# Row transfers sent without pauses, a shared chunk split around the first expert transposes, diagonal tiles made earlier

## The reference

```python
x = _layernorm(x + attention(x, Wq, bq, Wk, bk, Wv, bv, Wo, bo))     # x: (4, 512, 256)
router_logits = x @ w_gate                                          # 8 experts
probs = softmax(router_logits)
topk_w, topk_ids = top_k(probs, 2)
topk_w = topk_w / sum(topk_w)
gu = einsum('th,ehf->etf', x, w_gate_up)                            # w_gate_up: (8, 256, 256)
eo = einsum('eti,eih->eth', silu(g) * u, w_down)                    # g, u: the halves of gu
routed = einsum('te,eth->th', combine, eo)                          # two experts for each token
shared = (silu(x @ w_sh_g) * (x @ w_sh_u)) @ w_sh_down              # 512 inner columns
x = _layernorm(x + routed + shared)
```

## Time and profile before

| | before |
|---|---|
| median of 3 runs | 249.2 us (248.55 to 251.33) |
| the profiled execution: its time, its span | 249.33 us, 247.5 us |
| PE busy | 226.2 us (91%) |
| DVE busy | 148.7 us (60%) |
| POOL busy | 137.0 us (55%) |
| ACT busy | 116.2 us (47%) |
| PE's part of the chain that ended last | 81% |
| mean granted TensorE clock | 0.979 of 2.4 GHz |

### The profile page before, as it was taken

One profiled execution on the slowest core, in us unless ns is written; L12 is line 12 of the kernel. 1 busy time (PEld: TensorE's weight loads), 2 busy tenths in 40 slices (PEclk: granted clock), 3 DMA queues, 4 the chain that ended last, 5 costly groups with the idle time before them and its releaser, 6 DMA issues.

```text
span 247.5 us, 5128 instructions
## 1 busy us (share of the span) xinstructions
PE 226.2 (91%) x1440; PEld 195.1 (79%) x1440; DVE 148.7 (60%) x526; ACT 116.2 (47%) x298; POOL 137.0 (55%) x163
## 2 busy tenths in 40 slices
PE   7999999999899999999996699999999979999950
PEld 2578898798789889788994688888888867899950
DVE  2853462376555948659844666665666631699960
ACT  2272603932380731572342266776777752422460
POOL 0067688899788675566672045666656563003260
PEclk9999999999999999999999799999999999999995
DMA  5954763321411220221543235555555411982242
GB/s 169 371 180 109 229 196 83 97 82 39 127 47 43 88 87 0 88 84 65 205 162 82 69 113 166 148 160 153 166 162 150 131 51 11 381 214 79 86 162 93
DMA packets 21580, 31.72 MB, mean 128 GB/s; under 512 B 3248, under 2 KB 14257, under 8 KB 21556
## 3 DMA queue, kind: packets, MB, share of 16 engines
q1 hardware_dynamic: 17552, 22.46, 30.7%
q0 software_dynamic: 3456, 8.43, 9.9%
q10 hardware_dynamic: 548, 0.53, 0.6%
HBM read 19.70 MB, written 12.76 MB: 131 GB/s over the span
## 4 chain that ended last, share of the span: by engine, by line
PE 81%; DVE 8%; ACT 3%; issue 2%; DMA 2%; POOL 0%; POOLq 0%; DVEq 0%
PE bank L335 21%; PE bank L337 19%; PE bank L336 19%; PE bank L622 4%; PE bank L377 3%; PE bank L526 3%; DMA xt_raw<-in_xT 2%; PE bank L455 2%; PE bank L391 2%; PE bank L645 2%; PE bank L444 2%; PE bank L500 1%; PE bank L414 1%; PE bank L405 1%; PE bank L352 1%
## 5 line engine op out<-in xcount | busy, mean ns | idle before, releaser
L1404 POOL DMA_INDIRECT y_pairs<-x_t,dst x40 | 38.9, 973 | 36.9 <-DVE dst L1198 14.1
L1359 POOL DMA_INDIRECT x_slots<-x,slot x32 | 31.5, 984 | 15.9 <-DMA x_slots<-x,slot 7.7
L335 PE MATMUL bank<-wf_hi,ot_hi 128*128 x80 | 26.6, 333 | 2.4 <-DVE ot_lo L1200 1.9
L335 PE MATMUL bank<-x1t_hi,wf_hi 128*128 128x512 f32 x64 | 26.0, 407 | 0.7 <-DVE xt_raw L1052 0.5
L337 PE MATMUL bank<-x1t_hi,wf_lo 128*128 128x512 f32 x64 | 25.2, 395 | 0.0
L336 PE MATMUL bank<-x1t_lo,wf_hi 128*128 128x512 f32 x64 | 25.2, 393 | 0.0
L1340 POOL TENSOR_TENSOR wf_lo<-stage,wf_hi 128x512 fp32r<-128x512 f32 x18 | 23.1, 1284 | 1.4
L337 PE MATMUL bank<-wf_hi,ot_lo 128*128 x80 | 23.1, 289 | 0.0
L336 PE MATMUL bank<-wf_lo,ot_hi 128*128 x80 | 23.0, 287 | 0.0
L738 ACT ACTIVATE k_sb<-bank,cst 128x256 f32<-128x256 f32 x16 | 7.7, 480 | 30.6 <-PE bank L352 28.6
L1198 DVE SCALAR_TENSOR_TENSOR dst<-o_sb,te_f 128x1 f32 (+1 forms) x40 | 9.1, 226 | 21.0 <-ACT ot_hi L853 21.0
(11 more groups left out here) (181 smaller groups left out, 681.8 us busy)
## 6 DMA issues: line engine op xcount, KB each, us to landing
o_sb<-x_slots SPq DMA_DIRECT2D x40, 129.0 KB, 2.1
stage<-in_wffn SPq DMA_DIRECT2D x18, 256.0 KB, 2.7
x<-in_x SPq DMA_DIRECT2D x4, 512.0 KB, 6.7
out<-x SPq DMA_DIRECT2D x8, 256.0 KB, 2.1
xt_raw<-in_xT SPq DMA_DIRECT2D x3, 512.0 KB, 6.4
x_slots<-fill SPq DMA_DIRECT2D x9, 129.0 KB, 2.9
x<-in_watt SPq DMA_DIRECT2D x4, 256.0 KB, 6.2
k_sb<-y_pairs SPq DMA_DIRECT2D x2, 512.0 KB, 3.8
```

Source lines behind the costliest of these rows:

```text
L335: mm(o, w_hi, m_hi, start=start, stop=False, **more)
L1359: pool.indirect_dma_start(out=x_scat, out_offset=bass.IndirectOffsetOnAxis(ap=slot[:, j, t:t + 1], axis=0), in_=x1[:, t, :], in_offset=Non ...
L1404: pool.indirect_dma_start(out=y_scat, out_offset=bass.IndirectOffsetOnAxis(ap=dst[:, j:j + 1], axis=0), in_=ey[:, u, :], in_offset=None, b ...
```

## The change

Four things change.

- **POOL.** The function `landed` and its five calls are gone; all row transfers are issued one behind the other. `x1_norm(3)` and `x1_lo(2)` change places, and both second-half transfers of batch 1 now stand ahead of them.
- **PE.** The last shared chunk ahead of the experts, `shared_gu(2, 1)`, is split: part 0, then the transposes of tiles 0 and 1, then part 1, then tile 2's transpose. `e_gate_up(1)` and the wait for `sh_out` move ahead of tile 3's transpose. The ring's third and fourth tiles change PSUM banks, so that tile 2's transpose no longer writes a bank of that shared chunk.
- **ACT.** The silu and the rounding of that chunk stand between the roundings of tiles 1, 2 and the first silu; `e_silu(1)` moves ahead of the rounding of tile 3.
- **DVE.** The eight diagonal tiles are made between `shared_out(1, 0)` and `shared_out(1, 1)`; the chunk's multiplication and subtraction stand behind the remainders of tiles 1 and 2.

```diff
-            return bank[(4, 7, 3, 6)[u]][:, 0:KD * P]
+            return bank[(4, 7, 6, 3)[u]][:, 0:KD * P]
...
             shared_dn(1, 1)
-            shared_gu(2, 1)
...
             expert0, expert1, expert2 = experts_of(0)[RING - 1:]
+            shared_gu(2, 1, part=0)
             e_transposed(0, 0, 1)
             e_transposed(1, 1, 1)
-            pe.wait_ge(S["sh_out"], EARLY_B * CS + AHEAD)
+            shared_gu(2, 1, part=1)
+            pe.wait_ge(S["sres_out"], EARLY_B * 2)
             e_transposed(2, 2, 1)
             e_gate_up(0, 0, expert0)
-            pe.wait_ge(S["sres_out"], EARLY_B * 2)
+            e_gate_up(1, 1, expert1)
+            pe.wait_ge(S["sh_out"], EARLY_B * CS + AHEAD)
             e_transposed(3, 3, 1)
-            e_gate_up(1, 1, expert1)
             e_h_transposed(0, 0)
...
-            for c in range(AHEAD):
-                shared_sg(2, c)
-                shared_hh(2, c)
+            shared_sg(2, 0)
+            shared_hh(2, 0)
...
             e_x_hi(1, 1)
+            shared_sg(2, 1)
             e_x_hi(2, 2)
+            shared_hh(2, 1)
             e_silu(0, 0)
+            e_silu(1, 1)
             e_x_hi(3, 3)
-            e_silu(1, 1)
...
             shared_out(1, 0)
-            shared_out(1, 1)
-            shared_h(2, 1)
-            shared_lo(2, 1)
...
+            shared_out(1, 1)
             e_x_lo(0, 0)
             e_x_lo(1, 1)
+            shared_h(2, 1)
             e_x_lo(2, 2)
+            shared_lo(2, 1)
             e_h(0, 0)
+            e_h(1, 1)
             e_x_lo(3, 3)
-            e_h(1, 1)
...
             scatter(0, 1)
-            landed(0, 1)
             scatter(1, 0)
+            scatter(1, 1)
+            x1_norm(3)
             x1_lo(NB - 2)
-            x1_norm(3)
-            landed(1, 0)
-            scatter(1, 1)
-            landed(1, 1)
             scatter(2, 0)
-            landed(2, 0)
             scatter(2, 1)
-            landed(2, 1)
             scatter(3, 0)
             scatter(3, 1)
```

More of the change, by code:

```diff
@@ L1131, in weights, with e_x_lo, e_h, e_h_lo @@
                 dve.wait_ge(S["wtop_out"], 1)
+            def e_x_lo(j, u):
+                dve.wait_ge(S["xe_hi_out"], j + 1)
+                v.scalar_tensor_tensor(dst[:, bass.ds(j, 1)], xg[:, u, D + 1:DT], te_f[:, bass.ds(j + (RING - 1), 1)],
+                                       xg[:, u, D:D + 1], ALU.not_equal, ALU.add).then_inc(S["dst_out"], 1)
+                v.tensor_tensor(xe_lo[:, u, :, :], xe_bank(u).rearrange("p (k n) -> p k n", k=KD),
+                                xe_hi[:, u, :, :].bitcast(F32), ALU.subtract).then_inc(S["xe_lo_out"], 1)
+            def e_h(j, u):
+                dve.wait_ge(S["eg_out"], j + 1)
+                v.tensor_tensor(eh[:, u % 2, :], bank[u % 2][:, IM:2 * IM], eg[:, u % 2, :], ALU.mult
+                                ).then_inc(S["eh_out"], 1)
+            def e_h_lo(j, u):
+                dve.wait_ge(S["he_hi_out"], j + 1)
+                v.tensor_tensor(he_lo[:, u % 2, :], h_bank[:, 0:P], he_hi[:, u % 2, :].bitcast(F32),
+                                ALU.subtract).then_inc(S["he_lo_out"], 1)
             for b in range(NB - 1):
@@ L1361, in scatter @@
                                                 in_=x1[:, t, :], in_offset=None).then_inc(S[f"scattered{b}"], 16)
-            def landed(b, part):
-                pool.wait_ge(S[f"scattered{b}"], 16 * TOPK * (TB // 2) * (part + 1))
             split_x_lo(1)
```

## The result

| | before | after |
|---|---|---|
| median of 20 runs each | 249.34 us (248.5 to 251.74) | 248.55 us (246.85 to 249.92) |
| ratio of the two, 95% interval | | 0.9946 (0.992 to 0.9973) |
| the profiled execution: its time, its span | 249.33 us, 247.5 us | 248.62 us, 246.8 us |
| DVE busy | 148.7 us | 155.4 us |

VectorE was busy for 6.7 us more with the same 526 instructions, a first hint. The kernel became faster by 0.5%, some 1.3 us by the ratio (0.8 us between the medians, 0.7 between the two profiled executions), where 3.8 us were forecast; 248.55 lies above the range of 244.2 to 247.7. The lines of the changed kernel are shifted by about two: `ix_f` in `top_two` is line 1036 (before 1034), `hot` 1040 (1038), `slots` 1092 (1090), `x1_lo` 1348 (1346), the row transfers 1361 (1359), the tiles' transposes 621 (622), the mark 644 (645).

The account below looks back on a forecast made before the run. PE bounds nearly everywhere, but idles at the hand-over to the experts, on late tile loads and VectorE's chain. Moving the experts' first inner-product transpose from 141.19 to 137.36 gains 3.8 us: median 245.4 us, range 244.2 to 247.7.

Parts of the forecast that it names:

- the mark: PE's first transpose of an expert's inner product, at the experts' start: forecast to move from 141.19 to 137.36, 3.8 us.
- The step that failed: POOL, `x1_lo(2)` moved behind `x1_norm(3)`: 2.52 us long, ends at 100.9, wanted by nobody before ACT's copy; no cost.
- POOL's transfers: POOL without pauses: row transfers every 1.27 us; batch 3's first at 115.2 instead of 119.00, last starting at 124.1.
- the rival of stretched transfers: POOL: unpaused row transfers, stretched to 2.0 us each, hold up the last norm; 257 us; 4 in 100.
- The gate: SP's wait for pad and row transfers before the first tile loads: ends at 128.3 instead of 130.43, by the pads.
- The statement of the Trainium skill on HBM's load: SP's last pad, with less company, lands in about the shortest time, 2.0 us; sum some 0.9 us lower.
- The gate that doesn't move: SP's wait before the tile loads still ends at 130.4; reordering alone gives 1.7 us, 247.5 us; 12 in 100.
- PE and ACT at the hand-over: From the shared chunk to the experts: part 1 starts at 132.75, VectorE free 4.29 later, first expert inner-product transpose at 137.36.
- the clock rival: PE's clock stays low at the hand-over to the experts: about 0.9 us back, 246.3 us; 8 in 100.
- DVE's diagonal tiles: DVE between the two `shared_out(1)`: 1.57 us, from 128.55 to 130.1, free while DVE waits for PE until 130.14.
- that case: DVE without its wait before the second `shared_out(1)`: diagonal tiles cost their 1.57 us in front of the first remainder.
- The sum: Whole kernel: first transpose of an expert's inner product 3.8 us earlier, 249.33 to 245.5 us, expected median 245.4.

Follow-up runs that it names:

- the pads on two queues: Changed kernel with `x1_lo(2)` back ahead of `x1_norm(3)` and pad transfers of experts 4 to 7 issued by ACT: 247.07 us against 249.08 (0.9896); chip 3 ratio 1.03.

## Why the prediction was wrong, by its own steps

**The step that failed** is the sentence on POOL that `x1_lo(2)` "ends at 100.9 and is wanted by nobody" before ACT's copy. It ended at 98.26 + 2.55 = 100.81, as forecast, and nobody waited for its result. So its new place was priced at nothing, and no term of the sum stands for what it does to the instructions beside it. It held up `ix_f` and `hot` for 1.95 us; PE, which had 0.50 us of idle time there, got 1.78 more and ran at 1.2 GHz behind it. The trace divides the 3.26 us between `nw` and `slots(3)` in two: up to `slots(2)` (103.85 - 96.36 = 7.49 against 101.98 - 96.45 = 5.53) 1.96 us, and from there to `slots(3)` (14.17 against 12.87) 1.30, close to the 1.4 us that the low clock was seen to cost there. Everything behind is the forecast plus that, to within 0.2 us at the mark (140.80 - 137.36 = 3.44).

**The trace of before had shown it.** I had looked at `x1_lo(2)` in its old place only, where it runs beside an operation of VectorE with a PSUM input (L1016) and holds up nothing. Line 1034 for all four batches reads:

```profile
L1034 DVE CAST ix_f<-top_i x4: 172/184/1237, 59.7 to 111.9; 128x8 f32<-128x8 uint32 x4
```

A median of 184 ns and a longest of 1237. The longest is batch 0's. DVE there:

```profile
59.69 1.24 DVE L1034 CAST ix_f<-top_i 128x8 f32<-128x8 uint32 x1
60.97 0.64 DVE L1038 TENSOR_TENSOR hot<-cst,ix_f 128x32 f32<-128x32 f32 x2
61.64 1.21 DVE L1041 TENSOR_TENSOR hot_m<-hot 128x32 bf16<-128x32 f32 x1
```

and POOL:

```profile
59.62 1.28 POOL L1340 TENSOR_TENSOR wf_lo<-stage,wf_hi 128x512 fp32r<-128x512 f32 x1
60.85 0.61 POOL L1338 CAST wf_hi<-stage 128x512 fp32r<-128x512 f32 x1
61.54 1.26 POOL L1340 TENSOR_TENSOR wf_lo<-stage,wf_hi 128x512 fp32r<-128x512 f32 x1
```

Each group of VectorE's operations ends just behind the one of POOL beside it, and PE waited 1.21 us for `hot_m` there. In the Trainium skill, SBUF — State Buffer, section "Who interferes with whom", says that GpSimd shares a pair of SBUF ports with VectorE under an exclusive lock, and that a VectorE instruction with two SBUF inputs contends with a GpSimd instruction that reads SBUF; the later one waits for the whole of the earlier. The trace agrees for `hot` and `hot_m`, which read two operands in SBUF (1.33 us instead of 0.29, 1.21 instead of 0.19). `ix_f` reads only one, so that sentence doesn't cover it; it was held all the same, 1.11 us instead of 0.20. The prediction had weighed this page only in the other direction, VectorE against GpSimd's descriptors.

**POOL's transfers: right.** Batch 1's eight ran back to back from 85.65 to 95.46 (forecast 85.6 to 95.8). All 32 took 956 to 1262 ns, median 961, as before, so the rival of stretched transfers is refuted on this chip. Batch 3's first started 0.45 behind the start of its `slots` cast and the last 9.16 behind the first (forecast 0.35 and 8.9). In place of the pauses of the earlier trace rows POOL waits three times for `slots`, 8.1 us in all.

**The gate: right in kind, and its size held.** SP's line 294 took 28 ns instead of 1732: the wait ended at 131.6, by the last pad. The pads after:

```profile
L291 SPq DMA_DIRECT2D x_slots<-fill x8: 332/338/947, 119.9 to 129.0; - x8
...
DMA to landing us min/median/max: 2.6/3.1/3.4
```

The last pad landed 2.61 us behind its issue; I had taken 2.9. The statement of the Trainium skill on HBM's load (DMA: Bandwidth & Descriptors, "Latency and other measured facts") would have had it at the shortest time of before, 2.0; the trace doesn't agree. In the kernel with `x1_lo(2)` put back, it was 2.96. The gate that doesn't move is refuted: counted from `slots(3)`, the first load goes out 14.52 us behind it, before 16.48; forecast 14.35.

**PE and ACT at the hand-over: right**, to 0.02 us between part 1 and the mark. That closeness is part luck: VectorE was done with the chunk 4.38 us behind part 1's start (4.29 forecast), and the mark followed 0.25 behind that instead of 0.32. The granted clock was 1.00, so the clock rival is refuted there; a low clock came in another place.

**DVE's diagonal tiles: free, but not for the reason given.** The forecast put them into VectorE's wait ahead of the second `shared_out(1)`, 13.7 us behind the start of the cast of `slots(3)` (128.55 - 114.85). They ran 15.8 us behind it, at 133.83, for 1.65 us, and that wait was gone: VectorE had come late, held for 3.05 us in `w_top` (last section). As the forecast says for that case, they stood in front of the first remainder, which started at 136.12, though its rounding was ready at 135.54. It cost nothing because PE took up the first expert's gate and up only at 137.79.

**The sum.** Gain in the hand-over 26.34 - 22.78 = 3.56 us (forecast 3.8), lost ahead of it 3.26: 0.3 to 0.4 at the mark, 0.7 at the span's end. The two profiled executions differ by as much (249.33 - 248.62 = 0.71); the ratio of all the runs gives 1.3 us with an interval from 0.7 to 2.0, so the traces account for the lower end of it, and one trace of each can't say whether there is more. With the failed step taken out on the chip, the time is 246.37: inside the range, 1.0 us above the forecast. There the gain at the mark is (18.42 + 22.96) against (18.40 + 26.34) = 3.36, and 1.7 us of it are lost again behind the mark (108.0 against 106.3). The granted clock was 0.66 from 200 to 205 us there, where the kernel before and the one with the pads on two queues show 1.00. An estimate from that row: 5 x (1 - 0.66) = 1.7 us of full speed are missing. The low clock of the last stretch (225 to 244 us) is not the cause: it is 0.85 there and 0.82 with the pads on two queues, which loses nothing between the mark and the end. Why the clock fell at 200 us in the one kernel and not in the other stays open.

## What to carry to other kernels

Before an instruction is moved, look at what the other engines do where it lands, not only at who waits for its result; for POOL and VectorE, here, it depended on where VectorE's operands lay and on what the operation was. The cheapest way to see it is to ask for the shortest, median and longest duration of the neighbours: a small operation with a longest of over six times its median tells that something has already held it up once. Cut two traces at the same named events and compare the pieces: that shows in one row that a forecast gain was made and then lost elsewhere.

## What the hardware showed beyond this

- A POOL TENSOR_TENSOR of 128x512 in float32 with its inputs in SBUF (1.28 us) holds up VectorE's small operations on SBUF operands, a CAST with one input too (0.20 to 1.11 us). It does not hold up VectorE's operations with a PSUM input (line 1016 beside `x1_lo(2)` in the kernel before: 0.42 us each, as everywhere), nor BATCH_NORM_STATS2, which reads one SBUF operand (0.42 us in the same place, as everywhere). Once the pauses were gone, `w_top` (128x16), of two SBUF operands, came to stand beside the other `x1_lo` and took 3.05 us instead of 0.18, in all five traces of kernels without pauses from chips where the kernel before takes 249 us (3.04 to 3.05). By the records it began 0.46 ahead of POOL's two instructions (128.61, 2.55 us together) and ended 0.04 behind them; why an operation that began first was held isn't shown. It made VectorE late for the shared chunk (previous section), but no gain was lost by it at the mark.

```profile
93.10 0.42 DVE L1011 BATCH_NORM_STATS2 stat<-x 128x6 f32<-128x256 f32 x1
```

```profile
128.15 3.05 DVE L1132 TENSOR_TENSOR w_top<-wtmp,w_top 128x16 f32<-128x16 f32 x1
```

- Chips differ: the same kernel took 249 us on one and 265 to 266 on two others, and the same edit, no pauses, gave from no clear difference to 4% slower. Of the versions tried on each, `x1_lo(2)` put back has the lowest ratio on chip 1 (0.9854; with the pads on two queues, 0.9896, it can't be told apart), and the reordering with POOL's old pauses on chips 2 and 3 (0.9919 and 0.9886, the latter with an interval that holds 1). Not every version ran on every chip, but none of them was shown to be faster on all three.
